# Late shared units and the sums of their rows added in PSUM, gathers ahead of unit 7, expert pairs loaded one by one, three tiles between the stages of the routed loop

## What is computed

```python
x = layernorm(x + attn(x))      # 32 heads of 64, silu(qkv), decayed linear attention, RMS norm,
                                # sigmoid gate, output projection
x = layernorm(x + ffn(x))
# ffn, for all tokens:
shared = silu(x @ ws_gate) * (x @ ws_up) @ ws_down          # 256 -> 96 -> 256
ids, w = grouped top 6 of 64 experts (8 groups, 4 kept)     # scores = sigmoid(x @ gate_w) + bias
# each expert takes its first 48 tokens (CAP) in order, drops the rest
y[token] += w * down_e(silu(x @ w_gate_e) * (x @ w_up_e))
ffn = y + shared
```

## Time and profile before

| | us |
|---|---|
| median of 3 runs | 1367.67 (1365.44 to 1372.23) |
| profiled execution | 1362.8, its span 1361.0 |

### The profile page before, as it was taken

How to read it: one execution, slowest core, us unless ns; L and a number is a source line. 1 busy time by engine, 2 the same in 40 slices (tenths; PEclk the granted TensorE clock), 3 DMA queues, 4 the chain that set the end, 5 groups by cost and what they waited for, 6 DMA issues and landing times.

```text
span 1361.0 us, 39593 instructions
## 1 busy us (share of the span) xinstructions
PE 1291.1 (95%) x15260; PEld 1102.1 (81%) x15260; DVE 1029.9 (76%) x2327; ACT 927.8 (68%) x1746; POOL 493.1 (36%) x422
## 2 busy tenths in 40 slices
PE   7999999999999999999999999999999999978970
PEld 5788888888888888888888888888888888865550
DVE  6677878787878787888878787888787888753227
ACT  7667777777777677777777777777777777533434
POOL 0224233424232333324233423242333423335756
PEclk9999999999999999999999999999999999979995
DMA  8700000001000000000000000000000016558665
GB/s 297 261 2 10 27 9 27 9 3 32 2 26 9 26 10 26 9 27 9 26 9 27 9 13 23 10 26 17 27 17 26 17 38 197 158 170 244 107 195 203
DMA packets 47198, 81.11 MB, mean 60 GB/s; under 512 B 4464, under 2 KB 29136, under 8 KB 46160
## 3 DMA queue, kind: packets, MB, share of 16 engines
q1 hardware_dynamic: 37968, 65.58, 14.5%
q0 software_dynamic: 4608, 7.08, 3.0%
q10 hardware_dynamic: 4480, 6.29, 1.3%
HBM read 56.26 MB, written 22.68 MB: 58 GB/s over the span
## 4 chain that ended last, share of the span: by engine, by line
PE 85%; DVE 5%; DMA 4%; issue 3%; ACT 2%; POOL 1%; ACTq 0%; SPq 0%; DVEq 0%; POOLq 0%
PE pA L558 25%; PE pB L558 24%; PE pO L657 12%; PE pC L643 10%; PE pS L620 10%; DMA sums<-sb_stage,sb_sidx 3%; PE pC L558 1%; PE pS L558 1%; DVE sb_W L1195 1%; DVE sb_nmr L1654 1%; PE pC L682 1%; ACT sb_W L1174 0%; DVE sb_W L1642 0%; ACT sb_W L898 0%; POOL sb_stage L1738 0%
## 5 line engine op out<-in xcount | busy, mean ns | idle before, releaser
L1684 POOL TENSOR_TENSOR sb_vl<-sb_v,sb_vh 128x512 f16<-128x512 f32 x121 | 153.9, 1272 | 680.4 <-ACT sb_vh L944 680.4
L558 PE MATMUL pB<-sb_xh,sb_W 128*128 128x256 f16 x2048 | 349.6, 273 | 0.0
L1246 DVE TENSOR_TENSOR sb_S<-pS,sb_D 128x1024 f32<-128x1024 f32 x248 | 236.0, 952 | 120.5 <-PE pS L620 120.5
L952 ACT ACTIVATE sb_Shl<-sb_S 128x1024 f16<-128x1024 f32 x242 | 204.3, 844 | 110.9 <-DVE sb_S L1246 109.6
L558 PE MATMUL pB<-sb_xl,sb_W 128*128 128x256 f16 x1024 | 279.3, 273 | 0.0
L1252 DVE TENSOR_TENSOR sb_Shl<-sb_S,sb_Shl 128x1536 f16<-128x1536 f32 x121 | 225.4, 1863 | 10.4 <-ACT sb_Shl L952 10.1
L558 PEld LDWEIGHTS pB<-sb_xh,sb_W 128*128 128x128 f16 x2048 | 200.2, 99 | 22.8 <-issue 0.4
L558 PE MATMUL pA<-sb_xh,sb_W 128*128 128x256 f16 x1024 | 175.8, 274 | 10.2 <-DVE sb_W L1195 5.6
L558 PE MATMUL pA<-sb_W,sb_xh 128*128 128x256 f16 x1024 | 177.0, 275 | 3.7 <-ACT sb_qh L919 3.7
L657 PE MATMUL pO<-sb_Wo,sb_yh 128*128 128x256 f16 x1016 | 173.3, 273 | 0.0
L958 ACT ACTIVATE sb_gt<-pB 128x512 f32<-128x512 f32 x128 | 76.4, 597 | 140.9 <-PE pB L558 140.9
(11 more groups left out here) (290 smaller groups left out, 2711.9 us busy)
## 6 DMA issues: line engine op xcount, KB each, us to landing
sb_stage<-wprep SPq DMA_DIRECT2D x7, 1280.0 KB, 7.0
sb_W<-sums SPq DMA_DIRECT2D x16, 512.0 KB, 10.5
sb_W<-w_experts SPq DMA_DIRECT2D x17, 384.0 KB, 3.8
gather_rows<-sb_xr SPq DMA_DIRECT2D x16, 320.0 KB, 2.4
sb_xs<-xT SPq DMA_DIRECT2D x16, 256.0 KB, 2.9
sb_D<-decay SPq DMA_DIRECT2D x8, 512.0 KB, 7.9
sb_xn<-x SPq DMA_DIRECT2D x16, 256.0 KB, 3.0
sums<-sb_xr SPq DMA_DIRECT2D x16, 256.0 KB, 2.2
```

The lines of the kernel that those rows point to most:

```text
L558: last = nc.tensor.matmul(dst, a, m, start=(i == 0), stop=(i == len(terms) - 1), **kw)
L952: nc.scalar.activation(Sh[:, :, a:z_], S[:, :, a:z_], ACT.Copy).then_inc(s_Sh, 1)
L1246: nc.vector.tensor_tensor(scores_at(h)[:, :, a:z_], pS[:, :, a:z_], d[:, :, 0:z_ - a], ALU.mult).then_inc(s_Sm, 1)
L1684: nc.gpsimd.tensor_tensor(vl[q % 2][:, :, :], v32[:, :, :], vh[q % 2][:, :, :], ALU.subtract).then_inc(s_vl, 1)
```

## The change

- GpSimd: the product of unit 7 leaves the queue ahead of the gathers; VectorE takes products 7 to 11 (`BY_DVE`, new semaphore `s_usd`). Products 12 and 13 follow the last scatter, 14 and 15 follow `frs` 0 and 1. Two memsets go before `rstd1`.
- PE before the loop: the last `count` goes before unit 3's down, unit 5's down before the id matmuls, unit 7's gate-up between them and `spread_ids(0)`; `spread_ids(2)` moves into the loop. ACT: `running_counts` before unit 4's `unit_inner`. VectorE: `last_low_x1` first, then `spread_equals(0)`, product 7, `spread_equals(1)`.
- Loop: pass p does the transpose of p+1, gate-up p, inner transpose p-1, down p-2, merge p-3. `OUTBUF` is 6; `xgT`'s first two buffers move to `x1T` to make room.
- SyncE: pair p waits for p-18 downs, so one pair follows each tile's down, from the third to the thirteenth.
- End: all late gate-ups use banks `pA` and `pO`; `late_down(j)` writes unit j into a PSUM bank of its own (`pLate`) and leaves it open; `add_sums(c)` adds the two loaded regions to it by four matmuls with the identity once `s_fl[c]` is there. VectorE and ACT read chunks 8 to 15 from PSUM. `unit_keep`, GpSimd's adds and VectorE's adds for these chunks are gone.

```diff
-OUTBUF = 4
+OUTBUF = 6
...
-        xgT = carve(P, 2, NC * P)
-        xgT = [xgT[:, 0, :], xgT[:, 1, :]] + [v32[:, t, :] for t in range(NT)]
+        xgT = [x1T[:, t, :] for t in range(NC)] + [v32[:, t, :] for t in range(NT)]
...
-        late_sh = [y32[:, :], sq[:, :]] + [a[:, :, :].rearrange("p t n -> p (t n)") for a in (z, xn)] + ue
-        late_sh = [a.rearrange("p (k n) -> p k n", k=FIN) for a in late_sh]
...
+        pLateGU = [pA, pO]
+        pLate = [pB, pC] + [pS[:, i, :] for i in range(4)] + [pA, pO]
...
+        BY_DVE = range(UNITS_AHEAD - 1, UNITS_AHEAD + 4)
+        def shared_product(j):
+            if j in BY_DVE:
+                return s_usd, j - BY_DVE.start + 1
+            return s_ush, len([i for i in range(j + 1) if i not in BY_DVE])
...
+        def whole_rows(c, k):
+            if c >= UNITS_AHEAD:
+                return pLate[c - UNITS_AHEAD][:, k * HID:(k + 1) * HID]
+            return fin[c][:, 0, k, :]
...
-                sp.wait_ge(s_md, KINDS * ((p - RING) // 4 + 1))
+                sp.wait_ge(s_md, max(KINDS * ((p - RING) // 4 + 1), p - 18))
...
-                bank = pGU[j % 2]
+                bank = (pGU if j < UNITS_AHEAD else pLateGU)[j % 2]
...
-                pe.wait_ge(s_ush, j + 1)
+                pe.wait_ge(*shared_product(j))
...
+            def late_down(j):
+                pe.wait_ge(*shared_product(j))
+                pe.wait_ge(s_uact, j + 1)
+                for k in range(FIN):
+                    last = nc.tensor.matmul(pLate[j - UNITS_AHEAD][:, k * HID:(k + 1) * HID], us[0:FF, j % 2, k:T:FIN], wsd[:, :],
+                                            start=(k == 0), stop=False, skip_group_check=True)
+                last.then_inc(s_udn, 1)
+            def add_sums(c):
+                pe.wait_ge(s_fl[c], 16)
+                for k in range(FIN):
+                    for r in range(REGIONS):
+                        last = nc.tensor.matmul(pLate[c - UNITS_AHEAD][:, k * HID:(k + 1) * HID], ident[:, :], fin[c][:, r, k, :],
+                                                start=False, stop=(r == REGIONS - 1), skip_group_check=True)
+                last.then_inc(s_fp, 1)
...
             unit_gate_up(4)
-            unit_down(3)
             pe.wait_ge(s_th, SEQS)
             count(SEQS, STEPS)
+            unit_down(3)
             unit_gate_up(5)
...
             unit_gate_up(6)
+            unit_down(5)
             pe.wait_ge(s_ids, 1)
...
             nc.tensor.matmul(pC[:, 0:TILES], cand_rest[:, :], tile_rest, start=False, stop=True).then_inc(s_idp, 1)
+            unit_gate_up(7)
             pe.wait_ge(s_idx, 1)
             spread_ids(0)
+            unit_down(6)
             spread_ids(1)
-            unit_down(5)
-            unit_gate_up(7)
-            unit_down(6)
-            pe.wait_ge(s_eq, EQB)
-            spread_ids(2)
             unit_down(7)
...
-            for p in range(TILES + 1):
+            for p in range(TILES + 3):
+                if p + 1 < TILES:
+                    transpose_tokens(p + 1)
                 if p < TILES:
                     gate_up(p)
-                if p >= 1:
-                    down(p - 1)
-                if p + 1 < TILES:
-                    transpose_tokens(p + 1)
-                n = p + 3
+                n = p + 2
                 if n < TILES // EQB:
-                    pe.wait_ge(s_eq, n * EQB)
+                    pe.wait_ge(s_eq, (n if n > 2 else 1) * EQB)
                     spread_ids(n)
-                if p < TILES:
-                    transpose_inner(p)
-                if p >= 1:
-                    merge(p - 1)
+                if 1 <= p <= TILES:
+                    transpose_inner(p - 1)
+                if 2 <= p <= TILES + 1:
+                    down(p - 2)
+                if p >= 3:
+                    merge(p - 3)
+            pe.wait_ge(s_xgT, TILES)
             pe.wait_ge(s_mh, TILES)
+            pe.wait_ge(s_eq, TILES)
             pe.wait_ge(s_wo, TILES)
...
                     unit_gate_up(j + 1)
-                unit_down(j)
+                late_down(j)
+            for c in range(UNITS_AHEAD, FINALS):
+                add_sums(c)
...
-            def unit_keep(j):
-                act.wait_ge(s_udn, j + 1)
-                if j == UNITS_AHEAD:
-                    for i in range(UEV):
-                        act.wait_ge(s_ust[i], 16 * (UNITS_AHEAD // UEV))
-                nc.scalar.activation(late_sh[j - UNITS_AHEAD], pUD[j % 2][:, :].rearrange("p (k n) -> p k n", k=FIN),
-                                     ACT.Copy).then_inc(s_uev, 1)
...
+            running_counts(SEQS)
             unit_inner(4)
             unit_store(3)
-            running_counts(SEQS)
...
+                if t == 0:
+                    act.wait_ge(s_x1l, SEQS)
...
-            for p in range(TILES + 1):
-                if p < TILES:
-                    inner(p)
-                if p >= 1:
-                    weighted(p - 1)
+            for p in range(TILES + 2):
                 if p + 1 < TILES:
...
                 if p < TILES:
-                    evacuate_inner(p)
-            unit_inner(UNITS_AHEAD)
-            for j in range(UNITS_AHEAD, UNITS_AHEAD + 4):
-                unit_inner(j + 1)
-                unit_keep(j)
+                    inner(p)
+                if 1 <= p <= TILES:
+                    evacuate_inner(p - 1)
+                if p >= 2:
+                    weighted(p - 2)
+            for j in range(UNITS_AHEAD, SEQS):
+                unit_inner(j)
             for c in range(FINALS):
...
                 for k in range(FIN):
-                    last = nc.scalar.activation(fin[c][:, 1, k, :], fin[c][:, 0, k, :], ACT.Identity,
+                    last = nc.scalar.activation(fin[c][:, 1, k, :], whole_rows(c, k), ACT.Identity,
                                                 scale=frs[:, c % FACT, k:k + 1], bias=nmr[:, c % FACT, k:k + 1])
...
+            def unit_product(j):
+                dve.wait_ge(s_uact, j + 1)
+                nc.vector.tensor_tensor(us[0:FF, j % 2, :], us[0:FF, j % 2, :], uu[0:FF, j % 2, :], ALU.mult).then_inc(s_usd, 1)
             def last_low_x1():
...
                 place_rows(n)
-            for n in range(3):
-                spread_equals(n)
             last_low_x1()
+            spread_equals(0)
+            unit_product(UNITS_AHEAD - 1)
+            spread_equals(1)
             def evacuate(t):
...
                 nc.vector.tensor_copy(wo[:, t % OUTBUF, :], pM[:, 0:HID]).then_inc(s_wo, 1)
-            for p in range(TILES + 1):
+            for p in range(TILES + 3):
                 if p < TILES:
...
                     nc.vector.tensor_tensor(mh[:, p % 2, :], mhs[:, p % 2, :], pH[p % 2][:, FF:2 * FF], ALU.mult).then_inc(s_mh, 1)
-                if p >= 1:
-                    evacuate(p - 1)
-                if p + 3 < TILES // EQB:
-                    spread_equals(p + 3)
+                if p >= 3:
+                    evacuate(p - 3)
+                if p + 2 < TILES // EQB:
+                    spread_equals(p + 2)
+            for j in range(UNITS_AHEAD, UNITS_AHEAD + 4):
+                unit_product(j)
             for c in range(FINALS + 2):
-                if c < FINALS:
+                if c < UNITS_AHEAD:
                     dve.wait_ge(s_fl[c], 16)
-                    if c >= UNITS_AHEAD:
-                        dve.wait_ge(s_fp, c - UNITS_AHEAD + 1)
                     nc.vector.tensor_tensor(fin[c][:, 0, :, :], fin[c][:, 0, :, :], fin[c][:, 1, :, :], ALU.add).then_inc(s_fadd, 1)
...
                 if c < FINALS:
-                    dve.wait_ge(s_fadd, c + 1)
+                    if c < UNITS_AHEAD:
+                        dve.wait_ge(s_fadd, c + 1)
+                    else:
+                        dve.wait_ge(s_fp, c - UNITS_AHEAD + 1)
                     for k in range(FIN):
-                        last = nc.vector.bn_stats(st6[:, c % 2, k, :], fin[c][:, 0, k, :])
+                        last = nc.vector.bn_stats(st6[:, c % 2, k, :], whole_rows(c, k))
                     last.then_inc(s_fst, 1)
...
             nc.gpsimd.tensor_tensor(acc[:, 0:T], acc[:, 0:T], acc[:, T:2 * T], ALU.add).then_inc(s_fold, 1)
+            pool.wait_ge(s_C, STEPS)
+            nc.gpsimd.memset(v32[:, :, :], 0.0)
+            nc.gpsimd.memset(floats(qh[1])[0:FF, :], 0.0)
             pool.wait_ge(s_sse, SEQS)
...
             nc.gpsimd.tensor_tensor(rstd2[:, 0:NT], vv[:, 0:NT], mhalf[:, 0:NT], ALU.pow).then_inc(s_rstd2, 1)
-            pool.wait_ge(s_C, STEPS)
-            nc.gpsimd.memset(v32[:, :, :], 0.0)
-            nc.gpsimd.memset(floats(qh[1])[0:FF, :], 0.0)
-            for j in range(1, UNITS_AHEAD):
+            for j in range(1, UNITS_AHEAD - 1):
                 unit_product(j)
             def gather(p):
...
                 scatter(p)
-            for j in range(UNITS_AHEAD, UNITS_AHEAD + 5):
-                unit_product(j)
+            unit_product(UNITS_AHEAD + 4)
```

(21 more changed lines are left out.)

## The result

| | before | after |
|---|---|---|
| median, us | 1366.74 (4 runs, 1365.44 to 1372.23) | 1346.98 (4 runs, 1345.19 to 1347.06) |
| profiled span, us | 1361.0 | 1345.1 |
| first gather, first scatter | 1216.6, 1228.7 | 1207.1, 1231.9 |
| scatters 0 to 15, 15 to 23 | 59.0, 18.9 | 50.5, 19.6 |
| last landing L, end after L | 1310.6, 50.4 | 1305.9, 39.2 |

The ratio is 0.9845, 95% interval 0.9816 to 0.9873: 1.3 to 1.8% faster, 19.8 us by the medians. By the spans of the two profiles it is 15.9 us, as the profiled execution of before, 1362.8, is 3.9 us under its median: the first scatter 3.2 later, scatters 0 to 23 7.8 sooner, the end 11.2 shorter.

A forecast was written before the change was run, and what follows sets the result against it. After TensorE's full stretch to 1170 us no engine is full; token finding, routed loop and end bound it. Start 0, loop 4.1 and end 12.8 sum to 16.9 us off the 1367.67 median: 1350.8 us, range 1343 to 1359.

The forecast's parts named there:

- Start, (a): Finding the tokens, before the loop: first gather at 1207.2 us, 9.4 us earlier; tile 0 transposed at 1215.9 instead of 1219.84.
- Start, (b): Start of the routed loop: with three tiles between stages the first scatter comes at 1228.9 us, before 1228.69.
- nothing gained: Start of the loop: the gathers' head start is spent on PE's longer fill and GpSimd's waiting; bounds 2.5 us either way.
- Middle: Routed loop, scatters beside expert loads: single pairs lose 7 us instead of 10.7; bounds nothing and 10.7.
- the pair's DMA time: Middle of the loop: each expert pair's load takes 1.8 us of DMA time, as much as a tile.
- Drain: End of the loop: scatters 15 to 23 take 18.9 us, unaltered by six output buffers, then 3.9 us to landing.
- End: After the last landing L: DMA bounds the last chunks, end at L + 37.7 against L + 50.5, 12.8 us earlier.
- 1, single pairs for nothing: Loop's middle: single pairs cost nothing, each landing under 5.6 us; gain 24 to 26 us, 1343 us; chance 0.18.
- 2, half clock in the sums: End: PE stays at half clock, 3.5 us a chunk; only 5 us gained, 1363 us; chance 0.09.
- 3, starved scatters: Loop's middle: single loads hold every pair of scatters for 11.9 us; 9 us later, 1377 us; chance 0.05.
- 4, late units: Late units end after L + 25, or the fill is 10 us longer; gain 5 or less, 1364 us; chance 0.04.

The follow-up runs named there:

- again: The kernel after, unchanged, run once more on another chip; ratio 0.9867.
- noloads: The kernel after with the loads of pairs 21 to 31 cut to one row each, leaving out part of the weights; ratio 0.9835.
- singles: The kernel before with only the new load order, one expert pair per tile instead of four at a time; ratio 0.9962.
- endalone: The kernel before with only the change's new end (late units and sums in PSUM, products 8 to 15 moved); ratio 0.9920.
- bursts: The kernel after with its late expert pairs loaded four at a time again; ratio 0.9909.
- outbuf4: The kernel after with four output buffers in place of six; ratio 0.9860.
- inter: The kernel after with the last 16 chunks in alternating order (0, 8, 1, 9 ...) and product 14 moved earlier; ratio 0.9866.
- inter2: The kernel of inter with PE's sums of chunk 8 put ahead of the last unit's down; ratio 0.9866.
- hold: The kernel after with gathers 4 to 7 held until VectorE has written the first tile's product; ratio 0.9857.
- bursts_b: The kernel of bursts run once more on another chip; one run, profiled span 1350.5 us.

## Why the prediction was right, and where it was not

The forecast was 1350.8 us, with 16.9 us for the sum; the spans differ by 15.9, the medians by 19.8 (17.6 in again), and the median after, 1346.98, lies inside the range. Step by step:

- *Start, (a).* `gidx` at 1206.60 and the first gather at 1207.08 are as forecast. Tile 0's transpose at 1212.63 is 3.3 us earlier than the 1215.9 worked out: PE idled 0.92 us ahead of the id matmuls, where before had 3.37, its granted clock stayed at 1.00, and the half-clock spreads of the earlier trace rows weren't the row to take.
- *Start, (b).* The passes from the transpose to the first scatter were put at 13.0 us; without the stall they took 13.6 (noloads, 1213.07 to 1226.71). There "nothing gained" holds: 1226.7 against 1226.1 and 1226.3 in singles and endalone on the same chip, the transpose 4.3 us earlier and the lag 4.9 longer. In after the stall adds 5.6 us, the scatter is 3.0 us later than forecast and 0.5 outside the bounds of 2.5. Nothing in the trace of before shows this wait; it was missed.
- *Middle.* 7 us lost was the forecast, 2.8 came, well inside 0 to 10.7. The mechanism is right (bursts, singles, noloads); the mis-sized term is the pair's DMA time. In the 31 us from 1233.2 on, 8.9 tiles went through at a share of 1.03: 31.9 us of DMA time less 8.9 x 1.8 = 16.0 leaves 15.9 for 11 pairs, 1.45 us each, not 1.8. A pair's 576 KB at the 398 GB/s of the earlier trace rows are 1.48 us too, so that row was the better source. (The share of 1.07 that the forecast took for before's stretch is 1.04 in its trace.) Six buffers, on which the forecast let PE's pace rest, weren't needed (outbuf4).
- *Drain.* 19.6 against 18.9; in the other runs with three tiles of lag 18.2 to 18.5. In after one landing took 5.01 us with no load in flight. L at 1305.9, forecast 1306.4: the later start (+3.0), the better middle (-4.2) and the drain (+0.7) cancel. The right L is in part luck.
- *End.* 39.2 us after L, forecast 37.7, bounds 35.5 to 41. The last load near L + 30.2 fits: share over 1 to L + 29 in inter and L + 30 in after and inter2, and PE's last wait for a load ends at L + 28.3 and L + 29.5 in the latter two. What sets the end behind it is less plain than forecast: PE's sums in after, ScalarE's row of outputs in inter, load, PE's clock and outputs in turn in inter2, all within 1.0 us of each other. In after the tail from PE's last sum, 1338.8, to 1345.1 is 6.3 us, put at 5.7; PE's late start and low clock hold it 0.9 us more (sums done at L + 32.9, not 32.0).
- *Rivals.* 1, single pairs for nothing: wrong, but only 2.8 us from it in the middle. 2, half clock in the sums: true for the first chunk and a part of the second; PE then had 1.73 us of work a chunk and its clock came back (1.00 in 1330 to 1334). 3, starved scatters: the longest landing beside single pairs was some 7.3 us (hold), where a mean of 9.5 was the limit. 4, late units: no.

The rule of the Trainium skill weighed ahead (DMA: Bandwidth & Descriptors, Queues, rings and completion order) has the engines alternate between queues packet by packet. By it, the prediction said, single pairs would hold a scatter as long as bursts do. The runs have 7.6 to 9.7 us beside bursts and 6.6 to 7.3 beside single pairs, so what is queued does matter here; by which mechanism no run shows.

What stays open is the stall. That it follows the gathers is shown by hold, that it depends on the chip by bursts and bursts_b; what ScalarE waits for is not shown. Its own instructions are one candidate: the Trainium skill (Runtime: NRT & Kernel Launch, Instruction fetch mechanics) says that each engine fetches its program by DMA in blocks of 16 KiB, mostly hidden. The page of after has two queues for instructions, of 122 packets with 2.00 MB and 21 with 0.16; neither has a packet between 1212 and 1221 us, so no row shows a late block there. In after the DMA engines carry nothing for 1 us of ScalarE's second wait, which ends at 1220.19 (engines, granted clock, DMA share, GB/s):

```profile
1219.00:1219.50 0.50, 0.00 (x0) 0.00 (x0) 0.01 (x1) 0.00 (x0) 0.50 (x1) 1.00 0.01 0
1219.50:1220.00 0.50, 0.00 (x0) 0.00 (x0) 0.50 (x3) 0.00 (x0) 0.18 (x1) 1.00 0.00 0
```

That speaks against a transfer that ScalarE still waits for at that point, of instructions or else; in hold, where the wait ends at 1220.16, the DMA engines are busy.

## To carry to other kernels

When a queue of loads shares the DMA engines with transfers that others wait for, spread it to the pace of its use: against the 47.9 us of noloads, the same bytes in single pieces cost 2.6 to 4.0 us where bursts cost 9.2 to 11.3, since a wait counts only from the point where it passes the slack. Work that leaves three engines for a fourth that idles (here 24 passes over the last chunks) pays until the next resource is full, and then reordering helps little: read the DMA share before tuning the order. A deeper pipeline is paid in its fill, and what it buys is cover for delays that the trace of a good run doesn't show.
